# Finding the token of every slot: one matmul column per slot instead of three, and its tables made by two engines

## The chip, the cores and the metric

The kernel runs on one core of a Trainium2 chip. The metric is the device time of one execution in microseconds, as a median of several runs. In what follows PE is TensorE, DVE is VectorE, ACT is ScalarE, POOL is GpSimd and SP is SyncE, which here only issues DMAs.

## The reference

The input `x` holds 4 sequences of 512 tokens with 512 features each, 2048 tokens in all. Three layers follow one another:

```
x = x + 0.5 * ffn(layernorm(x))
x = x + attention(layernorm(x))      # 32 heads of 16, clip, q/k layernorm, linear bias, causal softmax
x = x + 0.5 * ffn(layernorm(x))

def ffn(x):                          # 8 experts, each token goes to the best 2
    logits = x @ W_gate + b_gate
    _, top_idx = top_k(logits, 2)
    y_all = relu(einsum('bsd,edh->bseh', x, W_e) + b_e)
    return mean(take_along_axis(y_all, top_idx[..., None], axis=2), axis=2)
```

Inputs, outputs and weights are float32.

## The kernel before

The program runs these stages one behind the other, with a barrier of all engines between two stages: `route_block` and `expert_block` of the first expert layer, `qkv_block`, `attention_block`, and `route_block` and `expert_block` of the second expert layer.

**Expert layer.** There are 2 x 2048 = 4096 pairs of a token and an expert. They are sorted by expert into tiles of 128 slots, each expert beginning a new tile, which gives at most 39 tiles (`SLOT_TILES`; `TAB` is 40). `expert_block` then goes over the 39 tiles: an indirect DMA of POOL gathers the 128 rows of the normalised tokens by `token_of[:, s]`, PE transposes them and multiplies them with the weights of the tile's expert, DVE adds the bias, ACT applies the relu, and an indirect DMA of POOL adds the rows to the accumulator in HBM at `row_of[:, s]`. A slot without a token reads some row and has a `row_of` of 2048 or more, which the DMA skips.

**`route_block`** makes these tables. Its first part goes over 16 tiles of 128 tokens: layer norm, transposes, the gate's logits, and beside them the loading and splitting of the expert weights into two parts (`ex.w_hi` by ACT, `ex.w_lo` by POOL, L1157). In the first layer PE also turns the weights of the next stage (`turn_wq`), and ACT copies them from PSUM (L1293). Its second part, which begins when all logits are there, is one serial chain of small DVE instructions. The helper `Chain` lets DVE wait for the end of each of them before the next (L1365 to L1443). It picks the two best experts, PE counts the ranks with matmuls by ones (L1234 to L1239), and DVE works out the slot of each of the 32 columns of tokens (16 tiles x 2 choices): `slot_hi` is the tile of slots and `slot_lo` the place in it.

**The inversion**, which the change touches, turns "slot of a token" into "token of a slot". DVE makes `at_tile`, a table of 32 x 3 x 40 bf16 numbers per partition: the one-hot of the slot's tile (L1411), the same times the partition number (L1413), and the same times the number of the token tile (L1414). For each of the 32 columns n it makes `at_col[n % 4]`, the one-hot 128 x 128 of the place in the tile (L1419, bf16, a ring of 4 buffers), and PE adds `at_col^T x at_tile[n]` into `id_ps`, 120 columns of PSUM (L1248). Each DVE instruction beyond the fourth waits for the matmul four before it. Behind the 32 columns DVE has eight instructions of one partition that make `expert_of` and `before_of` (L1422 to L1433), then it waits for the last matmul, and seven instructions (L1436 to L1443) turn the three sums per slot into `token_of` (partition + 128 x token tile) and `row_of` (the token, or 2048 + partition for an empty slot).

In the first layer PE has `turn_wq(4)` and `turn_wq(5)` in its queue behind the 32 matmuls, and ACT's last four copies (L1293) wait for them. The stage ends at a barrier, behind which POOL issues the first gather (L1475). POOL has nothing to do in the second part of `route_block` before.

Of the kernel before, what the change touches and what calls it, by code (L numbers as in the profile page):

```python
# [11 lines left out]
F32R = mybir.dt.float32r  # L12
BF16 = mybir.dt.bfloat16
I32 = mybir.dt.int32
U32 = mybir.dt.uint32
ALU = mybir.AluOpType
# [3 lines left out]
P = 128  # L20
D = 512
B, SEQ = 4, 512
TOKENS = B * SEQ
TILES = TOKENS // P
QT = SEQ // P
C = D // P
E = 8
# [888 lines left out]
TAB = SLOT_TILES + 1  # L916
# [40 lines left out]
def route_block(nc, prefix, ex, x_in, xn_dram, acc, w_gate, b_gate, w_e, b_e, o_dram=None, w_out=None, w_qkv=None, w_turned=None):  # L957
# [4 lines left out]
    with ExitStack() as ctx:  # L962
        m = Memory(nc, ctx, prefix)
# [15 lines left out]
        route_ps = m.ps("route_ps")  # L979
# [10 lines left out]
        TE2 = 2 * TE  # L990
        rank_ps, total_ps = route_ps[:, 0:TE2], route_ps[:, TE2:TE2 + 2 * E]
        id_ps = route_ps[:, TE2 + 2 * E:TE2 + 2 * E + 3 * TAB]
        COL_RING = 4
        n_expert = m.sb("n_expert", [P, TILES, E])
        n_full = m.sb("n_full", [P, E, TILES])
        n_col = m.sb("n_col", [P, P], BF16)
        n_tile = m.sb("n_tile", [P, TAB], BF16)
        n_token_tile = m.sb("n_token_tile", [P, 2 * TILES], BF16)
        n_part = m.sb("n_part", [P, 1])
# [18 lines left out]
        base = m.sb("base", [P, 2, E])  # L1018
# [8 lines left out]
        slot_lo_i = m.sb("slot_lo_i", [P, 2 * TILES], I32)  # L1027
        slot_hi = m.sb("slot_hi", [P, 2 * TILES, 1], BF16)
        slot_lo = m.sb("slot_lo", [P, 2 * TILES])
        at_col = m.sb("at_col", [P, COL_RING, P], BF16)  # L1030
        at_tile = m.sb("at_tile", [P, 2 * TILES, 3, TAB], BF16)
        found = m.sb("found", [P, 3, TAB])
        empty = m.sb("empty", [P, TAB])
# [7 lines left out]
        zeroed, ident_done, const_done = m.sem("zeroed"), m.sem("ident_done"), m.sem("const_done")  # L1041
# [10 lines left out]
        picked_done, rank_done, onehot_done, ids_done = (m.sem(n) for n in ("picked_done", "rank_done", "onehot_done", "ids_done"))  # L1052
# [83 lines left out]

        @block.gpsimd
        def _(pool):
            make_identity(nc, pool, ident, zeroed, ident_done)
            small = dict(base=0, allow_small_or_imprecise_dtypes=True)  # L1140
# [4 lines left out]
            nc.gpsimd.iota(n_token_tile[:, :], [[1, TILES], [0, 2]], channel_multiplier=0, **small).then_inc(const_done, 1)  # L1145
            nc.gpsimd.iota(n_part[:, :], [[0, 1]], channel_multiplier=1, **small).then_inc(const_done, 1)
            nc.gpsimd.iota(n_ring[:, 1:], [[16, RING_TURNS], [0, ADD_RING]], base=16, channel_multiplier=0,
                           allow_small_or_imprecise_dtypes=True).then_inc(const_done, 1)
# [6 lines left out]
            for n in range(TILES):  # L1155
                pool.wait_ge(w_hi_done, n + 1)
                nc.gpsimd.tensor_tensor(ex.w_lo[:, 2 * n:2 * n + 2, :], w_stage[n % 2][:, :, :],  # L1157
                                        ex.w_hi[:, 2 * n:2 * n + 2, :].bitcast(F32), ALU.subtract).then_inc(w_lo_done, 1)

        @block.tensor  # L1160
        def _(pe):
# [73 lines left out]
            for s in range(1, TILES):  # L1235
                last = nc.tensor.matmul(rank_ps[:, s * 2 * E:TE2], ones_bf[:, :], both[:, 0:TE2 - s * 2 * E], start=False,
                                        stop=(s == TILES - 1), skip_group_check=True)
# [8 lines left out]
            for n in range(2 * TILES):  # L1246
                pe.wait_ge(onehot_done, n + 1)
                nc.tensor.matmul(id_ps, at_col[:, n % COL_RING, :], at_tile[:, n, :, :].rearrange("p a s -> p (a s)"),  # L1248
                                 start=(n == 0), stop=(n == 2 * TILES - 1)).then_inc(ids_done, 1)
# [47 lines left out]
        def _(dve):  # L1297
# [31 lines left out]
            for u in range(PAIRS + 1):  # L1329
                p = u % 2  # L1330
# [37 lines left out]
            for k, source in enumerate((logits, rest)):  # L1368
# [5 lines left out]
                if k == 0:  # L1374
# [33 lines left out]
            chain(nc.vector.tensor_copy(slot_lo[:, :], slot_lo_i[:, :]))  # L1408

            every = [P, 2 * TILES, TAB]  # L1410
            chain(nc.vector.tensor_tensor(at_tile[:, :, 0, :], slot_hi[:, :, :].to_broadcast(every),  # L1411
                                          n_tile[:, :].rearrange("p (a s) -> p a s", a=1).to_broadcast(every), ALU.is_equal))
            chain(nc.vector.tensor_scalar(at_tile[:, :, 1, :], at_tile[:, :, 0, :], n_part[:, :], None, ALU.mult))  # L1413
            chain(nc.vector.tensor_tensor(at_tile[:, :, 2, :], at_tile[:, :, 0, :],  # L1414
                                          n_token_tile[:, :].rearrange("p (n a) -> p n a", a=1).to_broadcast(every), ALU.mult))
            for n in range(2 * TILES):
                if n >= COL_RING:
                    dve.wait_ge(ids_done, n - COL_RING + 1)
                nc.vector.tensor_scalar(at_col[:, n % COL_RING, :], n_col[:, :], slot_lo[:, n:n + 1], None,  # L1419
                                        ALU.is_equal).then_inc(onehot_done, 1)  # L1420
# [15 lines left out]
            chain(nc.vector.tensor_copy(found[:, :, :], id_ps.rearrange("p (a s) -> p a s", a=3)))  # L1436
            chain(nc.vector.scalar_tensor_tensor(found[:, 1, :], found[:, 2, :], float(P), found[:, 1, :], ALU.mult, ALU.add))
            chain(nc.vector.tensor_copy(ex.token_of[:, :], found[:, 1, :]))

            chain(nc.vector.tensor_scalar(empty[:, :], found[:, 0, :], -1.0, 1.0, ALU.mult, ALU.add))  # L1440
            chain(nc.vector.tensor_scalar(found[:, 2, :], empty[:, :], n_part[:, :], None, ALU.mult))
            chain(nc.vector.scalar_tensor_tensor(found[:, 1, :], empty[:, :], float(TOKENS), found[:, 1, :], ALU.mult, ALU.add))
            chain(nc.vector.tensor_tensor(ex.row_of[:, :], found[:, 1, :], found[:, 2, :], ALU.add))  # L1443
# [191 lines left out]
```

## Time and profile before

| what | value |
|---|---|
| median of 3 runs | 1092.69 us |
| lowest and highest run | 1081.46 and 1097.31 us |
| the profiled execution, its own device time | 1097.02 us |
| its span in the trace | 1095.3 us |
| PE busy | 894.9 us, 82% |
| DVE busy | 655.3 us, 60% |
| POOL busy | 434.6 us, 40% |
| ACT busy | 431.6 us, 39% |

The profiled execution is one run among several, and it took 4.3 us longer than the median of the others. Its span leaves out 1.7 us of the device time that lie around the first and the last instruction. Busy shares are averages over stages of very different kinds: the second part of `route_block` is only some 30 us long, twice in the program.

### The profile page before, as it was taken

How to read it: one execution, taken by the hardware profiler on the slowest of the kernel's cores; microseconds unless marked ns; L12 is line 12 of the kernel's file. 1: busy time of each engine (PE TensorE's matmuls, PEld its weight loads, DVE VectorE, ACT ScalarE, POOL GpSimd, SP SyncE). 2: the span in 40 equal slices, each digit the busy share in tenths (PEclk: the TensorE clock that was granted, in tenths of full speed). 3: DMA queues.
4: the chain of work that ended last, by engine and by line, in shares of the span. 5: the costliest groups of instructions: out<-in, count | busy, mean ns of one | idle time of the engine just before them, and what ended most of it. 6: DMA issues, size and time to landing. Idle time of an engine off the chain costs nothing. (4 is left out here: it accounts for less than half of the span.)

```text
span 1095.3 us, 20522 instructions
## 1 busy us (share of the span) xinstructions
PE 894.9 (82%) x6816; PEld 662.7 (61%) x6817; DVE 655.3 (60%) x1335; ACT 431.6 (39%) x754; POOL 434.6 (40%) x404
## 2 busy tenths in 40 slices
PE   4656799982898999839999999999668883699994
PEld 3555688862777777725555555555357672488873
DVE  6768244433866776717777777777148776444431
ACT  3332233331233333315777777777423330133321
POOL 4540677764267667620000000000023340477764
PEclk9997799996899999957999999999868895699997
DMA  7873577864235445874665656662066672278763
GB/s 243 297 235 118 165 147 147 148 123 80 75 115 173 150 141 176 213 192 101 149 143 132 138 129 139 132 141 73 24 209 231 236 259 100 66 140 149 147 132 48
DMA packets 127052, 163.12 MB, mean 149 GB/s; under 512 B 14161, under 2 KB 71633, under 8 KB 126705
## 3 DMA queue, kind: packets, MB, share of 16 engines
q1 hardware_dynamic: 109120, 124.89, 40.4%
q0 software_dynamic: 17856, 37.25, 18.3%
q8 instruction: 45, 0.74, 0.3%
q14 instruction: 31, 0.25, 0.1%
HBM read 98.48 MB, written 67.37 MB: 151 GB/s over the span
## 5 line engine op out<-in xcount | busy, mean ns | idle before, releaser
L885 DVE TENSOR_REDUCE att_part<-att_s_ps 128x2 f32<-128x1024 f32 (+2 forms) x160 | 195.7, 1225 | 71.5 <-PE att_s_ps L743 71.1
L851 ACT ACTIVATE att_prob<-att_st_ps 128x512 f32<-128x512 f32 x320 | 173.8, 595 | 84.3 <-PE att_st_ps L769 84.3
L143 PE MATMUL exp_z_ps<-ex_w_hi,exp_xT_hi 128*128 x312 | 133.6, 428 | 2.5 <-issue 1.7
L145 PE MATMUL exp_z_ps<-ex_w_hi,exp_xT_lo 128*128 x312 | 126.4, 405 | 0.0
L144 PE MATMUL exp_z_ps<-ex_w_lo,exp_xT_hi 128*128 x312 | 126.0, 404 | 0.0
L1540 ACT ACTIVATE exp_y<-exp_y 128x512 f32<-128x512 f32 x78 | 49.3, 632 | 185.8 <-DVE exp_y L1559 158.0
L1157 POOL TENSOR_TENSOR ex_w_lo<-ex_bias,ex_w_hi 128x1024 fp32r<-128x1024 f32 x32 | 75.8, 2370 | 111.5 <-ACT ex_w_hi L1273 111.4
L1547 DVE TENSOR_TENSOR exp_xT_lo<-exp_t_ps,exp_xT_hi 128x512 fp32r<-128x512 f32 x78 | 54.0, 692 | 108.0 <-ACT exp_xT_hi L1533 92.8
L707 POOL CAST att_m_parts<-att_part 128x28 fp32r<-128x28 f32 x32 | 6.6, 208 | 279.3 <-DVE att_part L889 279.3
L1475 POOL DMA_INDIRECT exp_xg<-xn,ex_token_of x78 | 78.2, 1003 | 91.9 <-SPq L1448 64.8
L782 PE MATMUL att_pv_ps<-att_prob,att_v_sb 128*32 128x256 f32 (+2 forms) x1280 | 103.1, 397 | 1.8 <-ACT att_oT L856 1.8
L1559 DVE TENSOR_TENSOR exp_y<-exp_z_ps,ex_bias 128x512 f32<-128x512 f32 x78 | 54.0, 692 | 75.4 <-PE exp_z_ps L145 70.0
L143 PE MATMUL qkv_o_ps<-qkv_w_hi,qkv_xT_hi 128*128 128x512 f32 x192 | 78.3, 408 | 1.7 <-issue 1.7
L145 PE MATMUL qkv_o_ps<-qkv_w_hi,qkv_xT_lo 128*128 128x512 f32 x192 | 75.7, 394 | 0.0
L144 PE MATMUL qkv_o_ps<-qkv_w_lo,qkv_xT_hi 128*128 128x512 f32 x192 | 75.6, 393 | 0.0
L1499 POOL DMA_INDIRECT acc<-exp_y,ex_row_of x39 | 62.0, 1590 | 31.2 <-DMA acc<-exp_y,ex_row_of 13.4
L1499 POOL DMA_INDIRECT out<-exp_y,ex_row_of x39 | 61.9, 1587 | 30.1 <-issue 13.1
L143 PEld LDWEIGHTS exp_z_ps<-ex_w_hi,exp_xT_hi 128*128 128x128 f32 x312 | 61.0, 195 | 17.3 <-issue 5.8
L1171 PE MATMUL route_t_ps<-route_ident,route_xn 128*128 128x128 f32 x128 | 27.8, 388 | 51.1 <-DVE route_xn L1355 51.1
L145 PEld LDWEIGHTS exp_z_ps<-ex_w_hi,exp_xT_lo 128*128 128x128 f32 x312 | 60.6, 194 | 14.4
L1513 PE MATMUL exp_t_ps<-exp_ident,exp_xg 128*128 128x128 f32 x312 | 49.0, 282 | 24.5 <-DMA exp_xg<-xn,ex_token_of 24.5
L722 PE MATMUL att_s_ps<-st_masks 64*128 64x256 bf16 (+1 forms) x640 | 58.3, 262 | 13.1 <-PEq L260 10.7
(202 smaller groups left out, 1835.1 us busy)
## 6 DMA issues: line engine op xcount, KB each, us to landing
ex_bias<-in_L_ffn_W_e SPq DMA_DIRECT2D x32, 512.0 KB, 5.8
xn<-route_xn SPq DMA_DIRECT2D x16, 512.0 KB, 5.0
v_vals<-qkv_vals SPq DMA_DIRECT2D x16, 512.0 KB, 2.8
q_parts<-qkv_turnedq SPq DMA_DIRECT2D x16, 512.0 KB, 3.8
k_parts<-qkv_turnedk SPq DMA_DIRECT2D x16, 512.0 KB, 5.4
att_v_sb<-v_vals SPq DMA_DIRECT2D x32, 256.0 KB
ex_bias<-in_L_attn_hidden_states SPq DMA_DIRECT2D x8, 512.0 KB, 4.1
acc<-ex_bias SPq DMA_DIRECT2D x8, 512.0 KB, 6.8
```

The lines of the kernel that those rows point to most:

```text
L143: nc.tensor.matmul(out, x_hi[:, s], w_hi(c), start=(c == 0), stop=False)
L144: nc.tensor.matmul(out, x_hi[:, s], w_lo(c), start=False, stop=False)
L145: last = nc.tensor.matmul(out, x_lo[:, s], w_hi(c), start=False, stop=(c == C - 1))
L722: nc.tensor.matmul(blocks_of(banks[half], where), mine[:, 0, :], rhs, start=(c == 0), stop=False, skip_group_check=True)
L782: last = nc.tensor.matmul(pv_ps[VW * h:VW * (h + 1), j * P + c0:j * P + c1], v_sb[n % RING][:, j, VW * h:VW * (h + 1)], prob[n % 2][:, col ...
L851: nc.scalar.activation(prob[n % 2][:, col:col + 512], st_ps[(e + half) % 3][:, :], ACT.Exp).then_inc(exp_done, 1)
L885: nc.vector.tensor_reduce(out, src, X_AXIS, ALU.max, negate=True).then_inc(red_done, 1)
L1157: nc.gpsimd.tensor_tensor(ex.w_lo[:, 2 * n:2 * n + 2, :], w_stage[n % 2][:, :, :], ex.w_hi[:, 2 * n:2 * n + 2, :].bitcast(F32), ALU.subtra ...
L1475: nc.gpsimd.indirect_dma_start(out=xg[s % RING][:, :], out_offset=None, in_=xn_dram[:, :], in_offset=bass.IndirectOffsetOnAxis(ap=ex.token ...
L1499: nc.gpsimd.indirect_dma_start(out=acc[:, :], out_offset=bass.IndirectOffsetOnAxis(ap=ex.row_of[:, s:s + 1], axis=0), in_=y[s % RING][:, : ...
L1547: nc.vector.tensor_tensor(xT_lo[r % 2][:, :], t_ps[r % 2][:, :], xT_hi[r % 2][:, :].bitcast(F32), ALU.subtract).then_inc(lo_done, 1)
L1559: nc.vector.tensor_tensor(y[r][:, :], z_ps[r % 2][:, :], ex.bias[:, bass.ds(expert * D, D)], ALU.add).then_inc(zb_done, 1)
```

## The change

The three numbers per slot become one. Each column's table `at_col` now holds, in the place of the slot, the token's number plus one instead of 1 (`n_token`), so that the sum in PSUM is the token plus one, or zero for an empty slot. The table by tile stays a plain one-hot and shrinks to 32 x 40 numbers. As numbers up to 2048 must pass exactly, both tables become float32 (F32R, the matmul's form for 4-byte operands) instead of bf16, and so does `n_col`. The instruction for a column has two operations, and both take their scalar from a column of SBUF. It is issued by DVE for even n and by POOL for odd n, each with a ring of three buffers of its own. `slot_lo` is followed by a semaphore `slots_done` for both engines instead of a link of the chain, and `at_tile` by `tiles_done`, for which PE waits once. The last seven instructions of DVE become four.

```diff
-        id_ps = route_ps[:, TE2 + 2 * E:TE2 + 2 * E + 3 * TAB]
-        COL_RING = 4
+        id_ps = route_ps[:, TE2 + 2 * E:TE2 + 2 * E + TAB]
+        COL_RING = 3
-        n_col = m.sb("n_col", [P, P], BF16)
+        n_col = m.sb("n_col", [P, P])
-        n_token_tile = m.sb("n_token_tile", [P, 2 * TILES], BF16)
-        n_part = m.sb("n_part", [P, 1])
+        n_token = m.sb("n_token", [P, 2 * TILES])
+        n_out = m.sb("n_out", [P, 1])
-        at_col = m.sb("at_col", [P, COL_RING, P], BF16)
-        at_tile = m.sb("at_tile", [P, 2 * TILES, 3, TAB], BF16)
-        found = m.sb("found", [P, 3, TAB])
+        at_col = [m.sb(f"at_col{i}", [P, COL_RING, P], F32R) for i in range(2)]
+        at_tile = m.sb("at_tile", [P, 2 * TILES, TAB], F32R)
+        found = m.sb("found", [P, TAB])
...
+        def column(engine, k, t):
+
+            n = 2 * t + k
+            if t >= COL_RING:
+                engine.wait_ge(ids_done, n - 2 * COL_RING + 1)
+            return engine.tensor_scalar(at_col[k][:, t % COL_RING, :], n_col[:, :], slot_lo[:, n:n + 1], n_token[:, n:n + 1],
+                                        ALU.is_equal, ALU.mult)
...
-            nc.gpsimd.iota(n_token_tile[:, :], [[1, TILES], [0, 2]], channel_multiplier=0, **small).then_inc(const_done, 1)
-            nc.gpsimd.iota(n_part[:, :], [[0, 1]], channel_multiplier=1, **small).then_inc(const_done, 1)
+            nc.gpsimd.iota(n_token[:, :], [[P, TILES], [0, 2]], base=1, channel_multiplier=1,
+                           allow_small_or_imprecise_dtypes=True).then_inc(const_done, 1)
+            nc.gpsimd.iota(n_out[:, :], [[0, 1]], base=TOKENS, channel_multiplier=1,
+                           allow_small_or_imprecise_dtypes=True).then_inc(const_done, 1)
...
+            pool.wait_ge(slots_done, 1)
+            for t in range(TILES):
+                column(nc.gpsimd, 1, t).then_inc(col_done[1], 1)
...
             for n in range(2 * TILES):
-                pe.wait_ge(onehot_done, n + 1)
-                nc.tensor.matmul(id_ps, at_col[:, n % COL_RING, :], at_tile[:, n, :, :].rearrange("p a s -> p (a s)"),
-                                 start=(n == 0), stop=(n == 2 * TILES - 1)).then_inc(ids_done, 1)
+                pe.wait_ge(col_done[n % 2], n // 2 + 1)
+                if n == 0:
+                    pe.wait_ge(tiles_done, 1)
+                nc.tensor.matmul(id_ps, at_col[n % 2][:, n // 2 % COL_RING, :], at_tile[:, n, :], start=(n == 0), stop=(n == 2 * TILES - 1)).then_inc(ids_done, 1)
...
-            chain(nc.vector.tensor_copy(slot_lo[:, :], slot_lo_i[:, :]))
+            nc.vector.tensor_copy(slot_lo[:, :], slot_lo_i[:, :]).then_inc(slots_done, 1)
 
             every = [P, 2 * TILES, TAB]
-            chain(nc.vector.tensor_tensor(at_tile[:, :, 0, :], slot_hi[:, :, :].to_broadcast(every),
-                                          n_tile[:, :].rearrange("p (a s) -> p a s", a=1).to_broadcast(every), ALU.is_equal))
-            chain(nc.vector.tensor_scalar(at_tile[:, :, 1, :], at_tile[:, :, 0, :], n_part[:, :], None, ALU.mult))
-            chain(nc.vector.tensor_tensor(at_tile[:, :, 2, :], at_tile[:, :, 0, :],
-                                          n_token_tile[:, :].rearrange("p (n a) -> p n a", a=1).to_broadcast(every), ALU.mult))
-            for n in range(2 * TILES):
-                if n >= COL_RING:
-                    dve.wait_ge(ids_done, n - COL_RING + 1)
-                nc.vector.tensor_scalar(at_col[:, n % COL_RING, :], n_col[:, :], slot_lo[:, n:n + 1], None,
-                                        ALU.is_equal).then_inc(onehot_done, 1)
+            nc.vector.tensor_tensor(at_tile[:, :, :], slot_hi[:, :, :].to_broadcast(every),
+                                    n_tile[:, :].rearrange("p (a s) -> p a s", a=1).to_broadcast(every),
+                                    ALU.is_equal).then_inc(tiles_done, 1)
+            dve.wait_ge(slots_done, 1)
+            for t in range(TILES):
+                column(nc.vector, 0, t).then_inc(col_done[0], 1)
...
             dve.wait_ge(ids_done, 2 * TILES)
-            chain(nc.vector.tensor_copy(found[:, :, :], id_ps.rearrange("p (a s) -> p a s", a=3)))
-            chain(nc.vector.scalar_tensor_tensor(found[:, 1, :], found[:, 2, :], float(P), found[:, 1, :], ALU.mult, ALU.add))
-            chain(nc.vector.tensor_copy(ex.token_of[:, :], found[:, 1, :]))
-
-            chain(nc.vector.tensor_scalar(empty[:, :], found[:, 0, :], -1.0, 1.0, ALU.mult, ALU.add))
-            chain(nc.vector.tensor_scalar(found[:, 2, :], empty[:, :], n_part[:, :], None, ALU.mult))
-            chain(nc.vector.scalar_tensor_tensor(found[:, 1, :], empty[:, :], float(TOKENS), found[:, 1, :], ALU.mult, ALU.add))
-            chain(nc.vector.tensor_tensor(ex.row_of[:, :], found[:, 1, :], found[:, 2, :], ALU.add))
+            chain(nc.vector.tensor_scalar(found[:, :], id_ps, -1.0, 0.0, ALU.add, ALU.max))
+            chain(nc.vector.tensor_scalar(empty[:, :], id_ps, 0.0, None, ALU.is_equal))
+            chain(nc.vector.tensor_copy(ex.token_of[:, :], found[:, :]))
+            chain(nc.vector.scalar_tensor_tensor(ex.row_of[:, :], empty[:, :], n_out[:, :], found[:, :], ALU.mult, ALU.add))
```

## Rows read from the trace of the kernel before

**Rows 1.** The page: the engine with the most busy time; the chain that ended last.

```profile
PE 894.9 (82%) x6816; PEld 662.7 (61%) x6817; DVE 655.3 (60%) x1335; ACT 431.6 (39%) x754; POOL 434.6 (40%) x404
...
DMA out<-exp_y,ex_row_of 0%
```

**Rows 2.** Two stretches: length; busy PE, PEld, DVE, ACT, POOL; clock; DMA.

```profile
99.00:104.50 5.50, 5.32 (x33) 3.51 (x34) 5.50 (x33) 0.00 (x0) 0.00 (x0) 0.50 0.00 0
...
930.00:935.50 5.50, 5.22 (x32) 3.33 (x32) 5.50 (x33) 0.00 (x0) 0.00 (x0) 0.50 0.01 1
```

**Rows 3.** Instructions in order of time, second layer, 926 to 941 us.

```profile
926.10 0.18 DVE L1408 CAST route_slot_lo<-route_slot_lo_i 128x32 f32<-128x32 int32 x1
926.32 1.49 DVE L1411 TENSOR_TENSOR route_at_tile<-route_slot_hi,route_n_tile 128x1280 bf16<-128x1280 bf16 x1
...
928.43 1.49 DVE L1414 TENSOR_TENSOR route_at_tile<-route_at_tile,route_n_token_tile 128x1280 bf16<-128x1280 bf16 x1
929.96 5.29 DVE L1419 TENSOR_SCALAR route_at_col<-route_n_col,route_slot_lo 128x128 bf16<-128x128 bf16 x32
...
930.28 5.32 PE L1248 MATMUL route_route_ps<-route_at_tile,route_at_col 128*128 128x120 bf16 x32 [8.32 <-DVE route_at_col L1419]
935.17 0.47 DVE L1422 TENSOR_TENSOR route_past<-route_ends,route_n_tile 1x320 f32<-1x320 f32 x1
...
938.01 0.28 DVE L1436 COPY route_found<-route_route_ps 128x120 f32<-128x120 f32 x1
...
939.52 0.20 DVE L1443 TENSOR_TENSOR ex_row_of<-route_found 128x40 int32<-128x40 f32 x1
940.98 1.07 POOL L1475 DMA_INDIRECT exp_xg<-xn,ex_token_of  x1 [34.59 <-SPq L1448]
```

**Rows 4.** Instructions in order of time, first layer, 99 to 110 us.

```profile
99.18 5.32 PE L1248 MATMUL route_route_ps<-route_at_tile,route_at_col 128*128 128x120 bf16 x32 [5.22 <-DVE route_at_col L1419]
...
107.14 1.08 ACT L1293 ACTIVATE wt_w_turned<-route_wq_ps 128x512 f32<-128x512 f32 x2 [0.26 <-PE route_wq_ps L1171]
...
108.42 0.20 DVE L1443 TENSOR_TENSOR ex_row_of<-route_found 128x40 int32<-128x40 f32 x1
109.89 1.17 POOL L1475 DMA_INDIRECT exp_xg<-xn,ex_token_of  x1 [30.20 <-SPq L1448]
```

**Rows 5.** Groups of DVE instructions by line and form: busy, mean ns.

```profile
L1355 DVE TENSOR_SCALAR route_xn<-ex_bias,route_mv,route_rstd 128x512 f32<-128x512 f32 x32 | 16.1, 544 | 0.6
...
L1419 DVE TENSOR_SCALAR route_at_col<-route_n_col,route_slot_lo 128x128 bf16<-128x128 bf16 x64 | 10.6, 252 | 0.1
```

**Rows 6.** Two DVE instructions of one size, in order of time.

```profile
938.79 0.18 DVE L1440 TENSOR_SCALAR route_empty<-route_found 128x40 f32<-128x40 f32 x1
939.01 0.24 DVE L1441 TENSOR_SCALAR route_found<-route_empty,route_n_part 128x40 f32<-128x40 f32 x1
```

**Rows 7.** Groups of POOL instructions by line and form.

```profile
L394 POOL TENSOR_TENSOR qkv_normk<-qkv_normk,qkv_lnp 128x512 f32<-128x512 f32 x16 | 20.7, 1292 | 1.3
...
L709 POOL TENSOR_TENSOR att_m_parts<-att_part,att_m_parts 128x28 fp32r<-128x28 f32 x32 | 7.8, 245 | 2.6
...
L207 POOL TENSOR_SCALAR_AFFINE_SELECT exp_ident<-exp_ident 128x128 f32<-128x128 f32 x2 | 0.6, 294 | 0.3
```

**Rows 8.** DVE and POOL at once, in order of time, 266 to 271 us.

```profile
266.67 0.98 POOL L369 MEMSET qkv_vals<- 128x512 f32 x2
266.76 0.98 DVE L556 CAST st_ident_r<-st_ident 128x128 fp32r<-128x128 f32 x1 [11.93 <-POOL st_ident L207]
...
268.03 2.29 DVE L552 TENSOR_TENSOR qkv_w_lo<-wt_w_turned,qkv_w_hi 128x2048 fp32r<-128x2048 f32 x1 [0.29 <-ACT qkv_w_hi L452]
...
268.60 1.87 POOL L376 TENSOR_SCALAR_AFFINE_SELECT st_masks<-st_masks 128x128 bf16<-128x128 bf16 x1
```

**Rows 9.** The gate's fp32r matmuls, second layer: first and last of fourteen.

```profile
910.21 0.36 PE L1196 MATMUL route_g_ps<-route_g_both,route_xT_hi 128*128 128x16 f32 x1
...
912.99 0.35 PE L1198 MATMUL route_g_ps<-route_g_both,route_xT_lo 128*128 128x8 f32 x1
```

More of the change, by code:

```diff
@@ L1051, in route_block @@
         ln_chain, chain_sem = m.sem("ln_chain"), m.sem("chain")
-        picked_done, rank_done, onehot_done, ids_done = (m.sem(n) for n in ("picked_done", "rank_done", "onehot_done", "ids_done"))
+        picked_done, rank_done, slots_done, tiles_done, ids_done = (
+            m.sem(n) for n in ("picked_done", "rank_done", "slots_done", "tiles_done", "ids_done"))
+        col_done = [m.sem(f"col_done{i}") for i in range(2)]
         wprep = load_transposed_weight(nc, m, w_out, C, wo_hi, wo_lo, ident, ident_done, t_ps + o_ps,
```

## The prediction

> **What bounds the kernel now.** I read the page first. PE is busy for 82% of the span, and the chain that ended last names only the final DMA, so the page doesn't say what one stage is worth [rows 1]. The change lies in two stretches of some 15 us, so I went on to the order of time. In both stretches every instruction of the inversion stands on DVE's line with gaps of 0.04 us, and PE, ACT and POOL only wait for it [rows 3, 4]. PE looks busy there (5.22 of 5.50 us), at a granted clock of 0.50, the 1.2 GHz level [rows 2], but this is one short matmul behind each DVE instruction. DVE's last instruction ends at 939.72, and POOL issues the first gather 1.26 us later [rows 3]; in the first layer 108.62 and 1.27 us [rows 4]. So in both layers DVE's chain ends the stage, and a microsecond taken from it is a microsecond of the kernel. In layer one a second chain runs close: PE's turned weights and ACT's copies end at 107.14 + 1.08 = 108.22, only 0.40 us earlier [rows 4]. It hangs on the end of the 32 matmuls.
>
> **Front of the chain.** L1413 and L1414 go: from the end of L1411, 926.32 + 1.49 = 927.81, to 929.96 it is 2.15 us, less one gap of 0.04, 2.11 us [rows 3]. L1411 stays: 1280 results per partition, 1.49 us. Its output becomes 4 bytes wide; its inputs, both tensors, are as before. 1280 elements at 1.49 us are slower than an element per ns, so I see no packing of 16-bit numbers to lose, and keep 1.49. The link behind L1408 goes too, some 0.1 us. POOL's first column waits for `slots_done` at 926.28 and finds L1411 running. DVE's columns begin at about 927.7 instead of 929.96: -2.2 us.
>
> **The columns.** Before, 32 of them took 5.29 us, 0.165 each [rows 3], though one lasts 252 ns [rows 5]: two neighbours overlap by some 0.087. Now they go in pairs, one of DVE and one of POOL, and PE takes them strictly in turn. The trace has no pair, so I bound its time p from four sides.
>
> - DVE alone: L1355 is the same instruction, two scalars from SBUF, for 512 fp32 elements: 544 ns [rows 5]. A scalar from SBUF costs 0.06 us (0.24 against 0.18 at 40 elements [rows 6]), so 544 - 120 - 180 leaves 0.24 for 472 elements more, about 0.52 ns per element. For 128 elements: 544 - 384 x 0.52 = 344 ns, less the overlap 0.26 us. Not the bound.
> - POOL alone: a one-input operation of 128 x 128 fp32 takes 294 ns; with two inputs the rows give 245 ns for 28 and 1292 ns for 512 elements, 2.16 ns per element, so 461 ns for 128 [rows 7]. A `tensor_scalar` of two operations isn't in the trace. I take 0.35 (one input, as in the row of 294, plus something for two scalars): 0.29 to 0.46.
> - PE: the operands are 4 bytes wide now. Thirteen steps of the gate's matmuls (same weights, 8 or 16 columns, same clock) take 912.99 - 910.21 = 2.78 us, 0.214 each [rows 9], where a bf16 step had at most 0.165. A pair can't be shorter than 0.43 us, whatever the others do, as long as the clock stays at 0.50.
> - DVE and POOL together: they disturb each other. The CAST of DVE, 128 elements, lasted 0.98 us beside two memsets of POOL and ended at 267.74, 0.09 us after them (267.65). POOL's L376, of the size of L207 (294 ns), lasted 1.87 us beside DVE's L552 and ended at 270.47, 0.15 us after it (270.32) [rows 7, 8]. So one waits for the other, but most of its start-up goes on beneath. If only the tails are exclusive, a pair costs about 0.09 + 0.06 x 2 for DVE and 0.15 to 0.29 for POOL, 0.36 to 0.50. If whole instructions are, 0.26 + 0.46 = 0.72.
>
> I take p = 0.50: above PE's floor of 0.43, with some friction. The range is 0.43 to 0.72. Rings of three buffers don't bind: a round of 0.35 for the column and 0.36 for the matmul, spread over three pairs, is 0.24.
>
> The Trainium skill has a rule that speaks against this change (page "SBUF — State Buffer", section "Who interferes with whom"): a DVE instruction in a two-port mode and a GpSimd instruction lock each other out for the whole instruction. The waits of rows 8 agree that they exclude each other; the tails of 0.09 and 0.15 us say that the exclusive part is shorter than the instruction. By the rule as it stands p would be 0.72, by the tails PE's floor decides.
>
> DVE is at most three pairs ahead of PE, so its sixteenth column ends 13 to 16 pairs after 927.7; I take 15, as POOL holds it back. That is 7.5 us at p = 0.50, against 5.29 - 0.08 before L1422 could start. +2.3 us.
>
> **Behind the columns.** The eight small instructions (935.17 to 938.01, 2.84 us [rows 3]) stay. They hide the rest of the matmuls: PE ends at most 3 x 0.72 = 2.2 us after DVE's last column. The last seven instructions took 939.72 - 938.01 = 1.71 us [rows 3]. Four remain: 0.20, 0.20, 0.18, and 0.26 for the one with a scalar from SBUF, with three gaps of 0.04: 0.96 us. -0.75 us.
>
> **Sum, layer two.** -2.2 + (15p - 5.2) - 0.75 = 15p - 8.2: at 0.50 -0.7 us; at p = 0.43 with 13 pairs -2.6; at 0.72 with 16 pairs +3.3.
>
> **Sum, layer one.** DVE's chain gives the same, ending at 107.9. But the wait for POOL's columns now stands in PE's queue before `turn_wq(4)` and `(5)`, and ACT's last copies wait for these. The first matmul starts at 99.18 - 2.2 = 97.0, the last ends at 97.2 + 16p, and from the end of the matmuls to ACT's end it is 108.22 - 104.50 = 3.72 us [rows 4]. So ACT ends at 100.9 + 16p: 108.9 at p = 0.50, +0.3 us against 108.62; at 0.43 -0.8; at 0.72 +3.8. Here the gain is lost to the second chain.
>
> SP's queue isn't touched: the bias load behind `wq_tr` (2 MB) is issued earlier or later with PE's turned weights, and is needed only by the first bias addition, behind the gather, the transposes and twelve matmuls of the experts. POOL's queue: the gathers stand behind the 16 columns, but also behind the barrier. The constants that POOL makes anew (two in the place of two, one with wider numbers) come at the start of the stage, ahead of its first L1157, which waits for ACT; I cost them at nothing, and at 0.3 us, one instruction of 128 x 128, if that cover were gone. The experts' part has the same tables and isn't changed.
>
> **Total.** -0.7 + 0.3 = -0.4 us on 1097.02: 1096.6 for an execution like the profiled one. This lay 4.3 us above the median, so the median becomes 1092.3. What a run differs by from another (1081.46 to 1097.31) is much more than the change moves, and about 2% is what a measurement of this kernel can tell from no change.
>
> **Rivals.**
>
> 1. *The engines take turns in full* (p = 0.72 or above). For it: every stall of rows 8. Against it: the short tails. It gives +3.3 and +3.8, so 1099.8; 'side by side' would then not be what happens, the columns being slower than DVE alone. The change turns from gain to loss at p = 0.55 in layer two and 0.48 in layer one. POOL's own instruction could be dearer than 0.46, as the trace doesn't have it: at 1.0 us, with DVE's tail 1.2, the layers would lose 10 and 12 us, some 1115.
> 2. *PE's clock rises* in this stretch, or the columns come without friction: p = 0.35. Then 15p - 8.2 is -2.9, and layer one is bound by ACT's end at 106.5 or DVE's at 105.7: -2.1. That is 1087.7. Against it: the row says 0.50 in both stretches with PE at 5.3 of 5.5 us.
> 3. *Nothing but the noise of the runs*: some other cause moves the median within the span of those shown.
>
> The Trainium skill prices a one-input GpSimd instruction as roughly line-rate (page "GPSIMD Engine Reference", section "4.1 Engine selection"); no row here shows a `tensor_scalar` of POOL, and by that rule p would stay at PE's floor, -3 us in all.
>
> **How the numbers follow.** Forecast (p 0.43 to 0.58, total -3 to +2 us): 0.55. Rival 1: 0.32, of which 0.05 for a POOL column near 1 us. Rival 2: 0.10. Something else: 0.03. The first alone spans 1089 to 1095; rival 1 reaches 1100, and the scatter of medians of three adds some 5 us on both sides of the likeliest. 1084 to 1102. Beyond 2% (1070.8 and 1114.5): faster 0.01, slower 0.04, the rest within.
>
> **What will show it.** POOL's column should last 0.3 to 0.5 us and DVE's about 0.34 where it isn't held up; many will be longer, ending just after one of the other engine. The distance of L1248's 32 matmuls, first to last, should be 8 us instead of 5.3. L1422 should start at the old time within 2 us, the last DVE instruction 0.75 us earlier after it. In layer one ACT's copies should end after DVE. Wrong would be: a POOL column over 0.6 us, PE at a clock of 1.00 in the stretch, or a stage longer or shorter elsewhere by over 5 us.

## The result and the profile after

The changed kernel is slower by a little under 1%: 1104.38 us against 1094.32 us (medians of 22 runs each), a ratio of 1.0082 with a 95% interval of 1.0047 to 1.0117. That is 9 us (5 to 13), where the forecast was no change (-0.4 us) and the range ended at 1102. Ratios and intervals leave out the runs over 1.5% above the fastest of their kernel; 18 of the 22 runs remain here and 17 of 22 before. The profiled execution of the changed kernel took 1092.34 us, *less* than the 1097.02 us of the one before. So the two pages can't be compared as wholes. The stretches show why. Cut at the first DVE instruction behind the rank matmuls (COPY `route_totals`), at the first gather and at the first instruction of `qkv_block` on POOL, the busy time by stretch of the kernel before reads as follows (length, then busy PE, PEld, DVE, ACT and POOL, the granted clock, DMA):

```profile
90.89:109.89 19.00, 11.46 (x64) 9.18 (x63) 16.59 (x66) 4.56 (x8) 0.00 (x0) 0.66 0.24 83
109.89:266.07 156.18, 133.97 (x624) 107.43 (x624) 53.97 (x78) 44.06 (x78) 104.71 (x87) 0.92 0.67 130
266.07:922.00 655.93, 560.70 (x5232) 389.88 (x5232) 453.64 (x876) 309.52 (x552) 185.13 (x199) 0.91 0.56 152
922.00:940.98 18.98, 5.32 (x32) 3.33 (x32) 16.58 (x66) 0.00 (x0) 0.00 (x1) 0.50 0.00 1
940.98:1095.30 154.32, 133.87 (x624) 107.45 (x624) 53.97 (x78) 44.05 (x78) 104.44 (x86) 0.92 0.65 121
```

and the changed kernel at the same events:

```profile
90.51:114.90 24.39, 16.67 (x64) 14.06 (x63) 14.28 (x45) 4.78 (x8) 14.35 (x16) 0.64 0.18 54
114.90:271.05 156.15, 132.15 (x624) 106.59 (x624) 53.96 (x78) 44.06 (x78) 104.76 (x87) 0.92 0.67 132
271.05:914.07 643.02, 555.86 (x5232) 384.92 (x5232) 444.53 (x876) 308.98 (x552) 185.23 (x199) 0.92 0.57 155
914.07:936.08 22.01, 10.03 (x32) 8.09 (x32) 13.82 (x45) 0.00 (x0) 14.84 (x16) 0.50 0.00 1
936.08:1090.60 154.52, 133.22 (x624) 105.78 (x624) 53.95 (x78) 43.94 (x78) 104.63 (x86) 0.93 0.65 121
```

The stretches with the inversion grew from 19.00 to 24.39 us and from 18.98 to 22.01 us, 8.4 us in all. The experts' stretches stayed within 0.2 us. The long stretch between them, which the change doesn't touch (attention and all that leads up to the second expert layer's logits), took 655.9 us in one profile and 643.0 us in the other, with the same counts of instructions. Such a difference of 13 us between executions is what the runs' scatter is made of, and it hides the change in any single run. In what follows the first measure is the length of the two inversion stretches. A second one runs on to the first transposes of the experts.

Inside the changed stretch of layer two, in order of time (the lines that answer to [rows 3]):

```profile
918.27 1.48 DVE L1427 TENSOR_TENSOR route_at_tile<-route_slot_hi,route_n_tile 128x1280 fp32r<-128x1280 bf16 x1
918.46 14.85 POOL L1144 TENSOR_SCALAR route_at_col<-route_n_col,route_slot_lo,route_n_token 128x128 fp32r<-128x128 f32 x16 [17.80 <-DVE route_slot_lo L1424]
919.67 1.19 DVE L1144 TENSOR_SCALAR route_at_col<-route_n_col,route_slot_lo,route_n_token 128x128 fp32r<-128x128 f32 x4
920.06 1.13 PE L1265 MATMUL route_route_ps<-route_at_tile,route_at_col 128*128 128x40 f32 x3 [6.03 <-DVE route_at_col L1144]
...
924.51 0.34 DVE L1144 TENSOR_SCALAR route_at_col<-route_n_col,route_slot_lo,route_n_token 128x128 fp32r<-128x128 f32 x1 [0.47 <-PE route_route_ps L1265]
924.67 0.61 PE L1265 MATMUL route_route_ps<-route_at_tile,route_at_col 128*128 128x40 f32 x2 [0.20 <-POOL route_at_col L1144]
...
930.49 0.47 DVE L1434 TENSOR_TENSOR route_past<-route_ends,route_n_tile 1x320 f32<-1x320 f32 x1
...
931.52 0.61 PE L1265 MATMUL route_route_ps<-route_at_tile,route_at_col 128*128 128x40 f32 x2 [0.52 <-POOL route_at_col L1144]
...
932.16 0.48 DVE L1442 TENSOR_TENSOR route_past<-route_mixed,route_n_tile 1x320 f32<-1x320 f32 x1
...
933.36 0.40 PE L1265 MATMUL route_route_ps<-route_at_tile,route_at_col 128*128 128x40 f32 x1 [0.43 <-POOL route_at_col L1144]
...
933.87 0.20 DVE L1448 TENSOR_SCALAR route_found<-route_route_ps 128x40 f32<-128x40 f32 x1 [0.51 <-PE route_route_ps L1265]
...
934.56 0.26 DVE L1451 SCALAR_TENSOR_TENSOR ex_row_of<-route_empty,route_n_out,route_found 128x40 int32<-128x40 f32 x1
936.08 1.14 POOL L1483 DMA_INDIRECT exp_xg<-xn,ex_token_of  x1 [2.77 <-SPq L1456]
```

DVE's line had gaps of only 0.04 us before. Now, from its sixth column on, DVE stands idle for 0.47 us before every column, released by a matmul, and PE stands idle for 0.20 us before nearly every pair, released by POOL. POOL alone has no gap: 16 columns in 14.85 us. The durations by tile (ns: least, median, most) say the same:

```profile
L1144 POOL TENSOR_SCALAR route_at_col<-route_n_col,route_slot_lo,route_n_token x32: 785/830/2064, 94.9 to 932.3; 128x128 fp32r<-128x128 f32 x32
L1144 DVE TENSOR_SCALAR route_at_col<-route_n_col,route_slot_lo,route_n_token x32: 337/346/429, 96.1 to 930.2; 128x128 fp32r<-128x128 f32 x32
```

A DVE column takes the 0.34 us that I had worked out. A POOL column takes 0.83, more than twice that. The POOL columns that run beside the two-input instructions L1434 and L1442 of DVE are longer still, 1.15 and 1.06 us, and the last matmul comes about half a microsecond later for it.

In layer one (answering to [rows 4]) the order of the ends has turned over:

```profile
94.91 14.35 POOL L1144 TENSOR_SCALAR route_at_col<-route_n_col,route_slot_lo,route_n_token 128x128 fp32r<-128x128 f32 x16 [16.55 <-DVE route_slot_lo L1424]
...
109.32 0.40 PE L1265 MATMUL route_route_ps<-route_at_tile,route_at_col 128*128 128x40 f32 x1 [0.16 <-POOL route_at_col L1144]
109.55 3.67 PE L1186 MATMUL route_wq_ps<-route_ident,ex_bias 128*128 128x128 f32 x16
...
111.09 0.26 DVE L1451 SCALAR_TENSOR_TENSOR ex_row_of<-route_empty,route_n_out,route_found 128x40 int32<-128x40 f32 x1
...
113.26 0.60 ACT L1309 ACTIVATE wt_w_turned<-route_wq_ps 128x512 f32<-128x512 f32 x1 [0.26 <-PE route_wq_ps L1186]
114.90 1.22 POOL L1483 DMA_INDIRECT exp_xg<-xn,ex_token_of  x1 [5.64 <-SPq L1456]
```

ACT's last copy ends at 113.86, 2.5 us after DVE (111.35), and the gather comes 1.04 us behind ACT. Before, DVE was the last by 0.40 us.

The change moves something behind the gather too. SP issues the load of the experts' bias (2 MB) as soon as PE's last turn is done, and it takes 7.8 us from issue to landing. The issue of the bias and PE's first transposes of gathered rows, in the kernel before:

```profile
107.61 0.34 SPq L1132 DMA_DIRECT2D ex_bias<-in_L_ffn_b_e  x1
...
115.66 1.94 PE L1513 MATMUL exp_t_ps<-exp_ident,exp_xg 128*128 128x128 f32 x8 [8.08 <-DMA exp_xg<-xn,ex_token_of]
```

and in the changed one:

```profile
113.25 0.34 SPq L1134 DMA_DIRECT2D ex_bias<-in_L_ffn_b_e  x1
...
121.48 1.94 PE L1521 MATMUL exp_t_ps<-exp_ident,exp_xg 128*128 128x128 f32 x8 [8.26 <-DMA exp_xg<-xn,ex_token_of]
```

The transposes wait for the first gather, and in both kernels they start 0.3 to 0.4 us after the bias load has landed (107.61 + 7.8 and 113.25 + 7.8). They come 5.77 us behind the gather before and 6.58 us in the changed kernel; in layer two, where that load was issued long before, it is 3.49 and 3.59 us. So layer one is another 0.81 us late there. At the end of the experts' stretch nothing of this is left (156.15 against 156.18 us), so it adds nothing to the 9 us.

### The profile page after: what moved, and what is told of

Its sections match the earlier page's. It is cut to its first block and busy times, and to the rows that moved or that the text cites. A ratio compares the mean times of both kernels' runs of the same rounds, so it can differ in the third digit from the quotient of the medians.

```text
span 1090.6 us, 20514 instructions
## 1 busy us (share of the span) xinstructions
PE 898.2 (82%) x6816; PEld 665.4 (61%) x6817; DVE 642.8 (59%) x1293; ACT 431.2 (40%) x754; POOL 464.3 (43%) x436
## 5 line engine op out<-in xcount | busy, mean ns | idle before, releaser
L144 PEld LDWEIGHTS exp_z_ps<-ex_w_lo,exp_xT_hi 128*128 128x128 f32 x312 | 60.3, 193 | 10.9
```

Of the source, the lines that this page charges most:

```text
L144: nc.tensor.matmul(out, x_hi[:, s], w_lo(c), start=False, stop=False)
```

## The experiments

Two theories stood against each other: **A**, the POOL column is dear by itself; **B**, POOL and DVE lock each other out, and a part of the 0.83 us is waiting. Most experiments edit only the inversion; one adds a block behind the kernel's end, and some move two weight turns of PE. In those that share out the columns anew, a list says which engine makes column n (0 is DVE, 1 is POOL), each engine has its own ring, and everything else follows from it:

```diff
+        COL_RINGS = (6, 1)
+        OWNER = [0 for n in range(2 * TILES)]
...
-                pe.wait_ge(col_done[n % 2], n // 2 + 1)
+                pe.wait_ge(col_done[OWNER[n]], NTH[n] + 1)
```

**All columns by POOL** (`OWNER` all 1, a ring of six).

> The changed kernel with all 32 columns made by POOL and none by DVE, so that nothing of DVE runs beside them. Measure: from the first DVE instruction behind the rank matmuls to the first gather of POOL, 24.39 us (layer one) and 22.01 us (layer two) in the changed kernel, 19.00 and 18.98 us before. Theory A, the POOL column is dear by itself: its step stays at 0.82 us, 16 more of them add 13 us to each layer, so about 37 and 35 us. Theory B, POOL and DVE take turns, and some 0.3 us of each 0.82 us is POOL waiting for DVE's column: the step falls to about 0.5 us, 32 of them take 16 us instead of 14.4, so about 27 and 24 us.

Measured: 36.26 us in layer one and 33.73 us in layer two (all pairs of lengths below are in this order). The tile's line:

```profile
L1147 POOL TENSOR_SCALAR route_at_col<-route_n_col,route_slot_lo,route_n_token x64: 781/787/2287, 93.0 to 970.1; 128x128 fp32r<-128x128 f32 x64
```

Theory A. With no DVE column anywhere near, a POOL column still takes 787 ns. Waiting for DVE is at most 0.04 us of the 0.83.

**All columns by DVE** (`OWNER` all 0, a ring of six).

> The changed kernel with all 32 columns made by DVE (one ring of six buffers), everything else as changed. Both theories: DVE's step is 0.26 us (344 ns less an overlap of 0.09), 8.3 us for 32. Against the kernel before: -2.2 us in front, +3.1 us for the columns, -0.75 us behind: about +0.2 us in layer two (19.2 us) and +0.5 us in layer one (19.5 us, ACT's copies last). So the kernel is within 1 us of the one before and about 8 us faster than the changed one. If the loss came from another place than the POOL columns (the 4-byte matmuls, say, at 0.4 us each instead of 0.214), it would stay.

Measured: 19.54 and 18.87 us, and a ratio to the kernel before of 0.9963 (0.9907 to 1.0020), which doesn't tell it from 1. The loss is gone as soon as POOL makes no column, with the 4-byte tables and the one number per slot kept. The columns took the 343 ns worked out:

```profile
L1147 DVE TENSOR_SCALAR route_at_col<-route_n_col,route_slot_lo,route_n_token x64: 340/343/347, 95.3 to 937.0; 128x128 fp32r<-128x128 f32 x64
```

**The last weight turns of PE in the middle.**

```diff
             for n in range(2 * TILES):
...
+                if w_qkv is not None and n in (8, 16):
+                    turn_wq(4 if n == 8 else 5)
-            if w_qkv is not None:
-                turn_wq(4)
-                turn_wq(5)
```

> The changed kernel with the last two weight turns of PE moved from behind the 32 matmuls to behind the 9th and the 17th. If the extra loss of layer one (24.39 against 22.01 us) is the queue of PE and ACT behind the matmuls, layer one falls to about 22.0 us and layer two stays: -2.4 us of the whole. If it has another cause, layer one stays at 24.4 us.

Measured: 22.31 us in layer one, 22.02 us in layer two. So 2.1 of the 5.4 us that layer one lost were the queue behind the matmuls: PE's last turns, then ACT's copies. The gain goes on behind the stretch. The bias load is now issued 7.5 us ahead of the gather, and the transposes come 3.69 us behind the gather instead of 6.58:

```profile
103.91 0.34 SPq L1134 DMA_DIRECT2D ex_bias<-in_L_ffn_b_e  x1
...
111.39 1.22 POOL L1482 DMA_INDIRECT exp_xg<-xn,ex_token_of  x1 [2.79 <-SPq L1455]
...
115.08 1.09 PE L1520 MATMUL exp_t_ps<-exp_ident,exp_xg 128*128 128x128 f32 x4 [6.03 <-DMA exp_xg<-xn,ex_token_of]
```

From the COPY to these transposes layer one takes 26.00 us against 30.97 in the changed kernel, 5.0 us less, and the experts' stretch is 1.0 us shorter (155.17 against 156.15). The ratio to the kernel before, 1.0111 (1.0024 to 1.0199, six runs), is too wide to show that; the stretches do.

**Forms of a POOL instruction, measured by themselves**, in a block of their own behind the kernel's end:

```diff
+            for form in FORMS:
+                for _ in range(REPEAT):
+                    run(form).then_inc(out, 1)
+                    n += 1
+                    pool.wait_ge(out, n)
...
+            for _ in range(12):
+                run("ptr2").then_inc(out, 1)
```

`REPEAT` is 4, and the last loop runs beside 32 instructions of the same form on DVE.

> The kernel before with a block behind its end in which POOL runs eight forms of one-input instructions, four of each and one after the other's end, with no other engine at work, and then twelve of the changed kernel's form while DVE runs 32 of the same form. Theory A: the changed form (fp32, 128 x 128, two scalars from SBUF, two operations) lasts 0.75 us or more alone. Theory B: 0.5 us or less alone, and 0.8 us beside DVE. Open in theory A is what makes it dear: if the two scalars, the forms with immediate numbers drop to about 0.35 us; if the second operation, the forms with one; if the number of elements, the one of 512 costs 4 times as much.

Measured, groups by line and form (busy, mean ns):

```profile
L1608 POOL TENSOR_SCALAR bench_dst<-bench_src,bench_sc 128x128 f32<-128x128 f32 x16 | 12.8, 799 | 1.6
L1616 POOL TENSOR_SCALAR bench_dst<-bench_src,bench_sc 128x512 f32<-128x512 f32 x4 | 8.3, 2069 | 0.4
L1621 POOL TENSOR_SCALAR bench_dst<-bench_src,bench_sc 128x128 f32<-128x128 f32 x4 | 3.2, 789 | 0.4
L1612 POOL TENSOR_SCALAR bench_dst<-bench_src 128x128 f32<-128x128 f32 x4 | 2.6, 642 | 0.3
L1610 POOL TENSOR_SCALAR bench_dst<-bench_src,bench_sc 128x128 f32<-128x128 f32 x4 | 2.4, 599 | 0.4
L1618 POOL TENSOR_SCALAR bench_dstb<-bench_srcb,bench_sc 128x128 bf16<-128x128 bf16 x4 | 2.4, 598 | 0.4
L1614 POOL TENSOR_SCALAR bench_dst<-bench_src 128x128 f32<-128x128 f32 x4 | 2.1, 527 | 0.3
L1620 POOL COPY bench_dst<-bench_src 128x128 f32<-128x128 f32 x4 | 1.2, 292 | 0.2
```

In this order: the changed form (two scalars from SBUF, two operations), the same over 512 elements, the same with max and add, two immediate numbers, one scalar from SBUF, the same in bf16, one immediate number, and a plain copy. Read as differences: a scalar from SBUF costs 0.07 us (599 - 527; 787 - 642 for two), a second operation with its immediate number 0.12 us (642 - 527), the width of the type nothing (599 and 598), and the step from a copy to one operation 0.24 us (527 - 292). No single thing makes it dear. The changed form costs (2069 - 789) / 384 = 3.3 ns for each element more, some 0.43 us for 128, and the other 0.36 us are fixed. How the three differences divide between the two parts wasn't measured. My bound of 0.29 was no more than the price of a copy: 292 ns, just as the row of 294. The least of the 16 is 784 ns and the most, the first beside DVE's stream, 890, so the neighbour costs 0.1 us at worst. DVE's 32 took 345 to 474 ns, median 347. Ten of them, one for each POOL instruction from the third on, took 470 ns or more and the others 354 or less: beside a POOL instruction one DVE instruction loses 0.12 us.

**The split alone**, in the kernel before: one-hot bf16 columns and three numbers per slot, but every second column by POOL, two buffers each.

```diff
+            return engine.tensor_scalar(at_col[k][:, t % COL_RING, :], n_col[:, :], slot_lo[:, n:n + 1], None, ALU.is_equal)
```

> The kernel before with one half of the change alone: the 32 columns are shared by DVE and POOL in turn, two bf16 buffers each, with the one-hot form of before (one scalar, one operation) and the three numbers per slot. Theory A, POOL's own time decides: its form lasts 0.60 us alone (measured behind the end of a kernel), 14 of 16 steps lie behind the tables by tile, 8.4 us instead of 5.3: stages of about 22.3 us in both layers (19.0 before), so the split by itself costs 3.3 us per layer. Rival, POOL is slow only in the fp32 form with two operations: a step of 0.35 us, stages of 19.0 to 19.3 us.

Measured: 22.79 and 21.77 us, 597 and 620 ns per POOL column (least and median). This is Theory A's case, as a step of 0.35 us would have given 19.0 to 19.3. So the split by itself costs 3.8 and 2.8 us even with the cheaper form. The other half of the change, which the run with all columns by DVE keeps, costs 0.5 and -0.1 us.

**Versions that might beat both.** fp16 holds whole numbers up to 2048, so the tables of the change, and `n_col` with them, can be 2 bytes wide (the lines removed are those of the run with all columns by DVE):

```diff
-        at_col = [m.sb(f"at_col{i}", [P, COL_RINGS[i], P], F32R) for i in range(2)]
-        at_tile = m.sb("at_tile", [P, 2 * TILES, TAB], F32R)
+        at_col = [m.sb(f"at_col{i}", [P, COL_RINGS[i], P], F16) for i in range(2)]
+        at_tile = m.sb("at_tile", [P, 2 * TILES, TAB], F16)
```

All columns by DVE, PE's turns in the middle:

> One number per slot as in the change, but all columns by DVE, with fp16 tables (which hold whole numbers up to 2048) instead of 4-byte ones, and the last two weight turns of PE behind the 9th and 17th matmul. If DVE's column follows the 16-bit form of before with one scalar more (252 + 60 ns, step 0.225 us), 32 take 7.2 us instead of 8.3: 17.8 us in both layers against 19.0 before, 2.3 us less in all. If the two-byte form saves nothing with two scalars (step 0.26), 18.9 us in both, equal to before.

Every fifth column by POOL (`OWNER = int(n % 5 == 4)`), PE's turns in the middle:

> As the run before it, but every fifth column (6 of 32) by POOL. Theory A: POOL needs 6 x 0.79 = 4.7 us, DVE 26 x 0.225 = 5.9 us, both at once; DVE is the slower and the stages take about 16.6 us, 4.8 us less than before in all and 1.2 us less per layer than with DVE alone. If the two lock each other out for whole instructions, the times add up to 10.6 us and the stages take 21 us.

The same two with PE's turns behind the matmuls, as in the change:

> The fp16 tables with all columns by DVE and PE's last turns behind the matmuls. Layer two 17.8 us as with the turns in the middle; layer one 17.9 us (ACT's end at 13.1 + 3.75 = 16.9 us, DVE's at 16.5) instead of 19.7. Against 19.0 before: 2.3 us less in all, 0.998. If POOL's six columns are worth what the traces say, this kernel is 2.6 us slower than the one with them.

> The fp16 tables with every fifth column by POOL, with PE's last two weight turns back behind the 32 matmuls. In layer one the turns in the middle held PE for about 2 us each with columns waiting; without them layer one should take what layer two took, 16.5 us, since ACT's copies then end at 11.8 + 3.75 = 15.5 us, near DVE's end at 15.2. Against 19.0 us before in both layers: 5.0 us less in all, a ratio of 0.995 to the kernel before. If layer one stays at 18.8 us, it wasn't the place of the turns.

| version | layer one, us | layer two, us | sum against before, us | the same to the first transposes, us | ratio to the kernel before (95%) | runs in the ratio |
|---|---|---|---|---|---|---|
| before | 19.00 | 18.98 | | | | |
| changed | 24.39 | 22.01 | +8.4 | +9.3 | 1.0082 (1.0047 to 1.0117) | 18 of 22 |
| changed, turns in the middle | 22.31 | 22.02 | +6.3 | +4.3 | 1.0111 (1.0024 to 1.0199) | 6 of 6 |
| all DVE, 4 bytes | 19.54 | 18.87 | +0.4 | +1.1 | 0.9963 (0.9907 to 1.0020) | 9 of 12 |
| all DVE, fp16, turns in the middle | 19.66 | 17.79 | -0.5 | -2.7 | 0.9904 (0.9836 to 0.9971) | 5 of 12 |
| a fifth POOL, fp16, turns in the middle | 18.80 | 16.47 | -2.7 | -4.7 | 0.9994 (0.9954 to 1.0034) | 12 of 12 |
| all DVE, fp16, turns behind | 18.19 | 17.80 | -2.0 | -1.3 | 0.9959 (0.9915 to 1.0003) | 11 of 12 |
| a fifth POOL, fp16, turns behind | 16.98 | 16.46 | -4.5 | -3.8 | 0.9887 (0.9796 to 0.9978) | 2 of 6 |

Layer two came within 0.15 us of every expectation of these four. Layer one came 1.9 and 2.2 us above it with the turns in the middle, 0.3 and 0.5 us above it with the turns behind. In the version with a fifth by POOL, both engines run at once and end together:

```profile
925.49 6.50 POOL L1148 TENSOR_SCALAR route_at_col<-route_n_col,route_slot_lo,route_n_token 128x128 f16<-128x128 f16 x6 [21.80 <-DVE route_slot_lo L1427]
926.69 5.89 DVE L1148 TENSOR_SCALAR route_at_col<-route_n_col,route_slot_lo,route_n_token 128x128 f16<-128x128 f16 x26
927.06 5.79 PE L1269 MATMUL route_route_ps<-route_at_tile,route_at_col 128*128 128x40 f16 x32 [6.01 <-DVE route_at_col L1148]
```

Here the two engines do disturb each other a little: of DVE's 26 columns in layer two five take 0.43 us, the others 0.30 or 0.31. It is nowhere near the 21 us that whole instructions in turn would have given.

I had expected the turns in the middle to be free inside the stretch, as with the changed kernel, and they weren't: once the columns come every 0.2 us, PE's turn holds up the ring. In the fp16 version with all columns by DVE (layer one):

```profile
96.96 1.94 PE L1190 MATMUL route_wq_ps<-route_ident,ex_bias 128*128 128x128 f32 x8
...
98.97 1.88 DVE L1148 TENSOR_SCALAR route_at_col<-route_n_col,route_slot_lo,route_n_token 128x128 f16<-128x128 f16 x8 [0.83 <-PE route_route_ps L1269]
```

DVE waits 0.83 us there, twice, and layer one takes 19.66 us; with the turns behind it takes 18.19. The same move was worth 2.1 us in the changed kernel, whose PE idled anyway. Yet behind the stretch the turns in the middle give something back. With them the transposes of layer one come 3.7 us behind the gather and the experts' stretch takes 154.5 to 155.2 us, in all three versions; with the turns behind the matmuls it is 5.8 to 6.6 us and 156.1 to 160.1 us, in all eight other profiles. So with a fifth by POOL the turns in the middle are the better place, by 0.8 us to the first transposes and 0.6 us to the end of the experts' stretch, though the inversion stretch is 1.8 us longer. The traces point at the bias load: behind the issue of the gather the DMA engines are idle with the turns in the middle (a share of 0.00 from 111.39 to 112.50 us in the changed kernel with that move), and busy with the load otherwise (0.90 from 109 to 111 us in the kernel before). No run moved that load by itself.

The traces put the two versions with a fifth by POOL first, 3.8 and 4.7 us (0.3 to 0.4%) below the kernel before when measured to the first transposes. The ratios can't confirm that order. The lowest, 0.9887, rests on two runs of six, and over all its runs the medians are 1095.00 against 1099.25 us, a ratio of 0.9961; the 0.9904 rests on five of twelve, and its medians are 1094.00 against 1093.43, 1.0005. The scatter of the long middle stretch, 641.5 us in the profile of all DVE with fp16 and turns in the middle and 659.4 us in that of its partner with a fifth by POOL, is larger than all the differences.

## Why the prediction was wrong

**What failed is one term of the sum**: "A `tensor_scalar` of two operations isn't in the trace. I take 0.35 (one input, as in the row of 294, plus something for two scalars): 0.29 to 0.46." It measured 0.79 alone and 0.82 to 0.83 in the kernel, so a pair took 0.82 us instead of the 0.50 forecast, and POOL's instruction set it, not PE. The row that I leaned on is a select, and on this engine no dearer than a copy (294 and 292 ns); a `tensor_scalar` with a single operation and one immediate number already takes 527. I took the two-input figure of 461 ns for an upper bound, and that simplest form lies above it. A step absent from the trace needed a bound on the other side too; rival 1 had one at 1.0 us, but with 5% and outside the range. A POOL column over 0.6 us stood among the signs of being wrong.

**The mechanism around the term held.** Put p = 0.82 into the sums of the prediction. Layer one, ACT's end at 100.9 + 16p: 114.0, 5.4 us later than 108.62; measured +5.39. Layer two, 15p - 8.2: +4.1; measured +3.03. There two misses partly cancel. DVE's sixteen columns took 13.3 pairs and not 15 (930.58 - 919.67 = 10.9 us), 1.4 us less. And DVE waited 0.51 us for PE behind the eight small instructions, where I had said that they hide the rest of the matmuls: at this p, with two POOL columns held up by those same instructions, they don't. Sum +8.4 in the traces, 9 in the runs.

**The bias load**, needed only by the first bias addition and put at nothing: right for the total, as the experts' stretch kept its length, but not for the reason given. The first gather came later with the load, by 0.81 us, and the run with the turns in the middle shows that an earlier load is worth something.

**Front** (-2.2 us): right. The first matmul came 6.0 us behind the COPY instead of 8.3, the 4-byte L1427 took 1.48 us.

**DVE's column** (344 ns alone, not the bound): right, 337 to 346 ns.

**PE's floor** (0.43 us per pair): the steps were 0.21 us (two matmuls in 0.61 us, one 0.40 long) at a clock of 0.50, and PE waited for POOL, so it wasn't the bound in the change. With all columns by DVE neither was it (32 columns in 8.3 us).

**The last instructions** (-0.75 us): right; from 933.87 to 934.82 is 0.95 us against 1.71 before, 0.76 us less.

**Engines that take turns**: not what happened between the columns. 787 ns without DVE and 830 ns beside it leave 0.04 us. The rule of the Trainium skill (page "SBUF — State Buffer", section "Who interferes with whom"), by which p would have been the sum of both instructions, isn't what these columns show: by it a DVE column would have waited for the POOL column running, and it lasted 0.34 to 0.35 us (0.43 at most) beside a POOL without gaps. Where DVE reads two tensors the exclusion is there: the first POOL column began at 94.91 beside L1427, lasted 2.06 us and ended at 96.97, 0.77 us after L1427. It isn't the cost of a first instruction: in the run with the split alone the second column too, beside L1429 with its two inputs, lasted 1.86 us. Of rival 1 only its last clause, a dearer POOL instruction, came true.

**Layer one's second chain**: foreseen with its formula, and the reason that layer one lost 2.4 us more than layer two within the stretch; moving the turns gave back 2.1.

**The range.** I had placed the scatter of runs at 5 us and the POOL column's uncertainty at 0.11 us per pair. The second was four times too small (0.82 - 0.35 = 0.47), and it is multiplied by about 16 in each of two layers.

## What to carry to other kernels

Before work is shared with another engine, the price of exactly that instruction on that engine has to be known: same operation count, scalars and size; a copy, a select or a two-input row of the engine is no bound for it. Where the consumer takes the shares strictly in turn, the slower engine sets the pace of both, so the shares have to be in the ratio of the speeds: with fp16 tables a fifth of the columns by POOL made layer two 1.3 us shorter than DVE alone (16.46 against 17.80), where one half by POOL, with 4-byte tables, made it 3.1 us longer (22.01 against 18.87). And when a chain that was just covered lies behind the same point (here PE's turns and ACT's copies, 0.40 us earlier), a delay costs there in full. The measure should reach past the stage that was changed: the place of PE's turns also decided when a load was issued, and with that went 2 to 3 us of the first gather behind the barrier.

## What the runs showed of the hardware that was unexpected

- POOL's `tensor_scalar` over 128 fp32 elements takes 527 ns with one immediate, 599 with one scalar from SBUF, 642 with two immediates and 787 with two scalars from SBUF; a copy of the same size takes 292. bf16 is no faster than fp32 (598 and 599). Each element more costs 3.3 ns in the two-operation form. The Trainium skill calls one-input work on this engine roughly line-rate (page "GPSIMD Engine Reference", section "4.1 Engine selection"); the copy's row leaves room for that, the arithmetic forms don't.
- A `tensor_scalar` of POOL disturbs one of DVE little, and is little disturbed by it: medians of 787 against 830 ns and of 343 against 346 ns. In a dense stream about one DVE instruction per POOL instruction takes 0.12 to 0.13 us more (470 to 474 ns instead of 347; with fp16 431 to 436 instead of 303). A two-input instruction of DVE holds a POOL column off while it runs (2.06 us for the first column, 1.15 and 1.06 beside L1434 and L1442).
- Where the first gather of 128 rows by indirect DMA was issued while a 2 MB load was under way (a DMA share of 0.90 from 109 to 111 us and 0.96 from 111 to 113 us before), PE could begin with its rows 5.8 to 6.6 us later. Where the DMA engines were idle it was 3.4 to 3.8 us.
- The same instructions of the stretch from attention to the second layer's logits take 641 to 643 us in two of the profiles and 651 to 659 us in the others, at a granted clock of 0.91 to 0.93. What decides that wasn't tried.
